# Three attention passes of one kernel: QKV signalled by halves, V rounded later, row-max work cut in half pieces with repeated products

## The reference, cut to what matters

```python
def fake_quant(x, bits=8):                      # per tensor
    qmax = 127.0
    scale = max(max(abs(x)) / qmax, 1e-8)
    return clip(round(x / scale), -128, 127) * scale

# quantised attention: B=8 batches, N=512 rows, 12 heads of 16
qkv  = fake_quant(x) @ fake_quant(w_qkv) + b_qkv
attn = fake_quant(softmax(fake_quant(q) @ fake_quant(k).T / 4))
out  = fake_quant(attn @ fake_quant(v)) @ fake_quant(w_proj) + b_proj
# routed stage, its attention: float32 throughout
q, k, v = layer_norm(x) @ qkv_w + qkv_b
x = x + softmax(q @ k.T / 4) @ v @ proj_w + proj_b
```

## Time and profile before

| | |
|---|---|
| median of 3 runs | 2557.32 us (2554.49 to 2562.55) |
| profiled execution | 2566.83 us |
| its span | 2564.8 us |
| PE busy | 1938.5 us, 76% |
| VectorE busy | 1504.3 us, 59% |
| ScalarE busy | 1058.4 us, 41% |
| GpSimd busy | 405.9 us, 16% |

### The profile page before, as it was taken

The page is one execution under the profiler, slowest core; times in us unless marked ns, Lnnn a source line. Parts: engine busy times, 40 slices in busy tenths (PEclk is TensorE's granted clock), DMA queues, the critical chain, the costliest instruction groups (busy, mean ns, idle before and its releaser), DMA issues. The chain is left out here.

```text
span 2564.8 us, 31153 instructions
## 1 busy us (share of the span) xinstructions
PE 1938.5 (76%) x9560; PEld 1006.8 (39%) x9560; DVE 1504.3 (59%) x2508; ACT 1058.4 (41%) x1847; POOL 405.9 (16%) x592
## 2 busy tenths in 40 slices
PE   5787888668785433777478865888899994899994
PEld 4555655444334110000111122333123332788883
DVE  6376389742104666999667773888968885111113
ACT  2002122132101356999678863222177761222221
POOL 5000000000111010111100003432003335122221
PEclk9899999766985665555589976777589996899997
DMA  3011100053991003333001004878767742565654
GB/s 79 18 31 37 48 23 25 2 223 125 410 411 42 0 0 124 119 119 119 28 16 36 25 1 68 131 96 107 93 75 96 99 59 77 178 212 194 212 195 183
DMA packets 147741, 265.16 MB, mean 103 GB/s; under 512 B 28618, under 2 KB 115883, under 8 KB 142636
## 3 DMA queue, kind: packets, MB, share of 16 engines
q1 hardware_dynamic: 135996, 242.54, 36.7%
q0 software_dynamic: 10480, 18.04, 2.1%
q10 hardware_dynamic: 1152, 3.15, 0.3%
HBM read 221.85 MB, written 57.71 MB: 109 GB/s over the span
## 5 line engine op out<-in xcount | busy, mean ns | idle before, releaser
L1654 PE MATMUL ps<-arena 128*128 x384 | 195.9, 615 | 121.7 <-DMA arena<-arena 62.2
L1688 ACT ACTIVATE ps<-ps,arena 128x512 f32<-128x512 f32 x384 | 256.6, 1451 | 7.7 <-POOL arena L1674 7.7
L2099 DVE TENSOR_REDUCE arena<-ps 128x1024 f32 x192 | 227.2, 1221 | 50.7 <-PE ps L2249 43.5
L1664 DVE TENSOR_REDUCE arena<-ps 128x1024 f32 x192 | 234.6, 1225 | 37.8 <-PE ps L1654 22.0
L1688 ACT ACTIVATION_READ_ACCUMULATOR ps<-ps,arena 128x1 f32 x384 | 239.7, 999 | 0.0
L2451 ACT ACTIVATE arena<-ps 128x1024 f32<-128x1024 f32 x192 | 185.2, 1021 | 95.8 <-PE ps L2333 94.6
L1838 ACT ACTIVATE arena<-ps 128x1024 f32<-128x1024 f32 x192 | 187.5, 1023 | 33.7 <-DVE arena L1860 29.4
L2781 DVE TENSOR_TENSOR arena<-ps,arena 128x384 f32<-128x384 f32 x39 | 21.7, 557 | 286.9 <-PE ps L2737 286.9
L2249 PE MATMUL ps<-arena 96*128 96x512 bf16 x384 | 159.6, 509 | 37.3 <-DVE arena L2099 24.6
L2761 ACT ACTIVATE arena<-ps,arena 128x256 f32<-128x256 f32 x234 | 89.5, 481 | 235.9 <-PE ps L2726 235.9
L528 PE MATMUL ps<-arena 96*128 96x456 f32 (+1 forms) x512 | 171.9, 486 | 8.7 <-DMA arena<-la_xt 5.1
(11 more groups left out here) (379 smaller groups left out, 3296.1 us busy)
## 6 DMA issues: line engine op xcount, KB each, us to landing
arena<-in_sm_w_dram SPq DMA_DIRECT2D x128, 576.0 KB
arena<-in_re_w_dram SPq DMA_DIRECT2D x39, 1252.0 KB, 6.0
arena<-ra_parts SPq DMA_DIRECT2D x192, 192.0 KB, 9.9
routed_in<-routed_in SPq DMA_DIRECT2D x8, 3332.0 KB, 13.8
ra_parts<-arena SPq DMA_DIRECT2D x48, 192.0 KB, 2.5
arena<-routed_in SPq DMA_DIRECT2D x39, 196.0 KB, 5.3
arena<-la_xt SPq DMA_DIRECT2D x16, 384.0 KB, 3.4
arena<-arena SPq DMA_DIRECT2D x64, 96.0 KB, 2.2
```

The costliest lines, as they stand in the source:

```text
L1654: ins = pe.matmul(ps[:, 2 * (n % 4) + t % 2, :], QM[j][:, h, t * P:(t + 1) * P], KI[:, b, h // HG, :], start=True, stop=True)
L1664: v.tensor_reduce(MXq[:, b, 2 * u:2 * u + 2, at_head(h)], ps[:, 2 * (n % 4):2 * (n % 4) + 2, :], AX.X, ALU.max).then_inc(s_lk, 1)
L1688: ins = act.activation(bank, bank, ACT.Exp, bias=nb[n % 4][:, t % 2:t % 2 + 1], scale=c_reg, accum_out=RS[:, b, t, at_head(h):at_head(h) + 1])
L2099: v.tensor_reduce(MX[:, bass.ds(b, 1), 2 * (n % 2):2 * (n % 2) + 2, n // 2].rearrange("p o t -> p (o t)"), ps[:, 2 * (n % 2):2 * (n % 2) + ...
```

## The change

Seven edits in the two stages.

1. *QKV.* The signal for q and k products counts two per batch, and PE's wait for free banks is per half. PE's order becomes q products, turn of b+1, k products, values, values. ScalarE scales the rows of b+2 between the copy of the turned rows and the store of k; two batches are scaled and rounded ahead of the loops. VectorE rounds b+2 after it has stored v.

```diff
-                qk.wait(act, b, 1)
+                qk.wait(act, b, k + 1)
...
             def batch(b, j, ahead):
-                if ahead:
-                    scale(b + 1)
                 store(b, 0)
                 if ahead:
                     turned(b + 1, 1 - j)
+                if ahead > 1:
+                    scale(b + 2)
                 store(b, 1)
...
-                ev.wait(pe, b, 0)
-                for s in range(2 * NG):
+                for k in range(2):
+                    ev.wait(pe, b, k - 1)
+                    for s in range(NG * k, NG * k + NG):
...
+                    ins.then_inc(qk.sem, 1)
+                    if ahead and k == 0:
+                        turn(b + 1)
                 values(b, j, 0)
-                if ahead:
-                    turn(b + 1)
                 values(b, j, 1)
```

```diff
+    tq, rq = Signal(nc, "qa_scaled", 3, 0), Signal(nc, "qa_rounded", 4, 1)
...
+                for n, (j, src, bias, k) in enumerate(((0, QF, magic, 0), (0, KF, magic_k, 1), (1, QF, magic, 0))):
+                    if n == 0:
+                        rq.wait(act, i, 0)
+                    elif n == 2:
+                        rq.wait(act, i, 1)
+                    act.activation(TM[n % 2], scaled(src, 2 * i + j), ACT.Identity, bias=bias,
+                                   scale=inv2[:, k:k + 1]).then_inc(tq.sem, 1)
...
+                v.tensor_scalar(TM[2], scaled(KF, 2 * i + 1), inv2[:, 1:2], magic_k, ALU.mult, ALU.add).then_inc(s_kt, 1)
```

```diff
+                Hb = m.H[:, b, :, :]
+                v.tensor_tensor(Hb, Hb, bp[:, None, :].to_broadcast([P, T, D]), ALU.add)
+            ex.wait(v, B - 1, N1)
+            l = Link(v, s_a)
+            l(v.tensor_reduce(pmax, RS, AX.XYZ, ALU.min))
+            v.reciprocal(pmax, pmax).then_inc(s_b, 1)
```

```diff
+    def shift_rows(eng, groups, done):
+        for q in groups:
+            for g in range(NG):
+                row, at = 32 * q + HD, 3 * (q * NG + g)
+                eng.dma_start(QI[row:row + 3, :, g, :], BT[at:at + 3, :, :]).then_inc(done, 16)
...
+            for b in range(2, B):
+                v.wait_ge(s_vt, b + 1)
+                round_v(v, b, TV[:, b, :].rearrange("p (h d) -> p h d", d=HD))
```

```diff
+            def pieces(b):
+                turns = [(turn, b + 1, c, half) for c in range(NC) for half in range(2)] if b + 1 < B else []
+                return [(product, b, s, half, c) for s in range(2 * NC) for half in range(2) for c in range(NC)] + \
+                    [(values, b, t) for t in range(2)] + turns + [(values, b, t) for t in range(2, T)]
+
+            def scores(b, j, n, again):
                 h = n // 2
                 mx.wait(pe, b, n - 1)
-                for t in (2 * (n % 2), 2 * (n % 2) + 1):
+                first = 2 * (n % 2)
+                for t in (first, first, first + 1) if again else (first, first + 1):
                     ins = pe.matmul(ps[:, t, :], ST_[j][0][0:KR, h, t * P:(t + 1) * P],
                                     ST_[j][1][0:KR, h, :], start=True, stop=True)
                 ins.then_inc(u1.sem, 1)
...
+                work = pieces(b + 2) if ahead else []
                 for n in range(NU):
-                    scores(b, b % 2, n)
-                    if ahead and 0 < n <= len(pieces):
-                        piece, *which = pieces[n - 1]
-                        piece(b + 2, *which)
+                    scores(b, b % 2, n, n < len(work) and work[n][0] is not values)
+                    if n < len(work):
+                        piece, *which = work[n]
+                        piece(*which)
...
+                act.activation(Vb[:, :, :, 1, :], m.one.to_broadcast([P, T * NH * HD]).rearrange(
+                    "p (t h d) -> p t h d", t=T, h=NH), ACT.Copy)
+                ins = act.activation(ST_[b % 2][1][KR:KR + 3, 3 * (b // 2):3 * (b // 2) + 3, :], m.one[KR:KR + 3].to_broadcast(
+                    [3, 3 * S]).rearrange("p (h s) -> p h s", h=3), ACT.Copy)
```

More of the change, by code:

```diff
@@ L1379, in _ @@
             pool.memset(WPf, 0.0).then_inc(s_z, 1)
+            pool.memset(magic_k, MAGIC)
+            pool.memset(above, MAGIC + 1.0)
             pool.memset(BQ, 0.0).then_inc(s_z, 1)
@@ L1496, in _ @@
             round_x(0)
-            with v.Fori(0, B - 1) as b:
+            round_x(1)
+            with v.Fori(0, B - 2) as b:
                 batch(b, True)
-            batch(B - 1, False)
+            for b in range(B - 2, B):
+                batch(b, False)
             v.wait_ge(s_lk, B)
@@ L1601, in _ @@
                 pool.memset(QM[j].rearrange("p h s -> p (h s)").bitcast(F32), 0.0).then_inc(s_qz, 1)
-        @block.sync
-        def _(sp):
-            sp.wait_ge(s_on, 1)
-            rq.wait(sp, B - 1, 3)
-            for j in range(HG):
-                rows = slice(32 * j + HD, 32 * j + HD + 3)
-                sp.dma_start(KI[rows].rearrange("p b g s -> p b (g s)"),
-                             ones[0:3, None, :].to_broadcast([3, B, NG * S])).then_inc(s_one, 16)
     RS, MXq = g3(P, [B, T, NH]), g3(P, [B, T, NH])
@@ L1617, in quantised_attention @@
     mark = g3.at
+    s_a, s_b, s_c, s_ln, s_bp, s_bt, s_bc, s_q = (sem(f"qa_shift_{n}") for n in (
+        "chain", "max", "max_of_all", "log", "parts", "turned", "copied", "rows"))
     nb = [g3(P, [2]) for _ in range(4)]
@@ L1697, in quantised_attention @@
     rows = lambda a: a.rearrange("p b t h -> p (b t) h")
-    s_a, s_b, s_c, s_ln, s_bp, s_bt, s_bc, s_q = (sem(f"qa_shift_{n}") for n in (
-        "chain", "max", "max_of_all", "log", "parts", "turned", "copied", "rows"))
+    s_q2 = nc.alloc_semaphore("qa_shift_rows_pool")
+    TV = QF.rearrange("p b g s -> p b (g s)")[:, :, 0:T * D]
     km = [sem(f"qa_k_spread{j}") for j in range(2)]
@@ L1741, in _ @@
                            ps[0:3 * NH, 2:4, :].bitcast(BF16), ACT.Copy).then_inc(s_bc, 1)
+            for b in range(2, B):
+                act.activation(TV[:, b, :], VF[:, b, :, :].rearrange("p t d -> p (t d)"), ACT.Identity, bias=magic,
+                               scale=inv2[:, 2:3]).then_inc(s_vt, 1)
         @block.tensor
@@ L2027, in _ @@
             v.wait_ge(s_w, 16 * (5 + HG))
-            v.memset(XT[DC:DC + 1, 0, :], 1.0)
+            for j in range(2):
+                v.memset(XT[j][DC:DC + 1, 0, :], 1.0)
         @block.scalar
@@ L2236, in values @@
                     rows = DC + 1 - c
-                    ins = pe.matmul(ps[:, 6 + t // 2, t % 2 * D:(t % 2 + 1) * D], XT[0:rows, c, t * P:(t + 1) * P],
-                                    W[0:rows, c, 2 * D:3 * D], start=(c == 0), stop=(c == NC - 1))
+                    ins = pe.matmul(ps[:, banks(b, 0) + t // 2, t % 2 * D:(t % 2 + 1) * D],
+                                    XT[b % 2][0:rows, c, t * P:(t + 1) * P], W[0:rows, c, 2 * D:3 * D],
+                                    start=(c == 0), stop=(c == NC - 1))
                 if t == T - 1:
                     ins.then_inc(qp.sem, 1)
-            pieces = [(turn, c) for c in range(NC)] + [(product, s, c) for s in range(2 * NC) for c in range(NC)] + \
-                [(values, t) for t in range(T)]
-            def scores(b, j, n):
+            def pieces(b):
[3 more added lines that the diff above has]
+            def scores(b, j, n, again):
                 h = n // 2
                 mx.wait(pe, b, n - 1)
-                for t in (2 * (n % 2), 2 * (n % 2) + 1):
+                first = 2 * (n % 2)
+                for t in (first, first, first + 1) if again else (first, first + 1):
                     ins = pe.matmul(ps[:, t, :], ST_[j][0][0:KR, h, t * P:(t + 1) * P],
@@ L2269, in batch @@
                             ins.then_inc(s_bt, 1)
+            for c in range(NC):
+                for half in range(2):
+                    turn(0, c, half)
             for b in range(2):
-                for piece, *which in pieces:
-                    piece(b, *which)
+                for piece, *which in pieces(b):
+                    piece(*which)
             for b in range(B):
```

176 lines of the change are left out of this document (90 added, 86 removed).

## The result

| | before | after |
|---|---|---|
| median of runs, us | 2559.94 (2554.49 to 2562.74, 4 runs) | 2474.34 (2473.01 to 2478.28, 4 runs) |
| span of the profiled execution, us | 2564.8 | 2473.2 |

The ratio is 0.9671, 95% interval 0.9655 to 0.9688: 3.3% faster. The forecast was 2487, range 2468 to 2516. The sum of -70 us was 15 too small; the median fell by 85.6 and the profiled span by 91.6 us.

A forecast was written before the change was run, and what follows sets the result against it. No engine was taken to bound the whole; stages were bound by chains or single engines. Terms -19 - 5.5 - 8 + 0.5 - 5 - 8 - 25.5 + 0.4 gave -70 us: 2487 as median, range 2468 to 2516.

The forecast's parts named there:

- QKV: QKV of the quantised attention: signalling products per half breaks the PE/ScalarE chain, leaving the longest engine; -19 us (-24 to -12).
- I take 7.6, at today's clock: QKV period per batch, down from 10.34 us: PE's 6.41 busy plus the gap between value products and hand-offs.
- What is late next is PE's own work: QKV after the change: PE itself, needing 7.6 us per batch with hand-offs, sets the period.
- Quantising and ones rows: Quantising loop's shorter chain, -5.5 us, and ones rows made by rounding bias, not issued by SP, -8: -13.5.
- Pass 1: Bias add moved here, eight VectorE adds of 0.96 us mostly absorbed by slack and ScalarE's queue: +0.5 (0 to +7.7).
- Shift block: Earlier GpSimd reconfiguring gains 1.3 us, twelve DMAs split over two queues, roundings of V added: -5 us (0 to -7).
- Projection: Projection loop loses the bias add and a short wait, period about 3.05 us: -8 us (-6 to -8.5).
- Routed pass: Routed row-max pass: halved pieces in all units, VectorE sets 28.8 us per batch; -25.5 us, memset +0.4.
- Rival 1: Clock stays at 1.2 GHz in the routed pass, so repeated products cost time: +47, 2604 us; chance 0.04.
- rival 2: Routed pass gains less: PE sets 1.30 us per unit, 32.4 per batch, -5 instead of -25.5: 2508 us; chance 0.15.
- rival 3: Small gains don't add up in QKV, shift block, bias add and quantising: 19 us less, 2506 us; chance 0.11.
- Rival 4: Memsets and moved waits give nothing, repeats cost a little: whole kernel within 0.3% of before; chance 0.02.

The follow-up runs named there:

- the third variant: Changed kernel without repeated score products in routed-pass batches 0 to 5, but with both score products repeated in batches 6 and 7: 2490.46 us, ratio 0.9705.

## Why the prediction was right, and where its sizes were off

**QKV (-19, measured -24.0).** The mechanism held: blocks of six products, ScalarE waiting 0.30 us for PE. The step "I take 7.6, at today's clock" was mis-sized. It let PE's 6.41 us set the period, and those were measured at 0.67. Once the chain was gone the clock was 1.00 in most of the stage, PE needs 4.08 there, and the period is 6.50; batches that ran partly at the lower level take up to 7.50, and only in those is the forecast's PE (busy 6.66) the longest engine. I had worked out VectorE's "6.6 to 7" and used it only as a bound. The variant with the short k maximum confirmed that VectorE is next, and ScalarE right behind it. "What is late next is PE's own work" was wrong for the batches at 1.00.

**Quantising and ones rows (-13.5, measured -14.8).** The pair's 6.91 us is the 6.9 of the chain. The ones rows gave 10.1 instead of 8: the four spreads take 3.12 us of issue, and with their landing and the block change 5.65 us in all, where I had left 7.6. The loop gave the other 4.7 instead of 5.5. The 5.5 was not the sum of its own terms, which is 4 x (8.92 - 6.9) - 3.5 = 4.6.

**Pass 1 (+0.5, measured +1.0).** With the add taken out again it is 0.6 to 1.4 shorter. ScalarE's records (line 1711) have a median of 1146 ns instead of the 1622 of the earlier trace rows, and 1622 again without the add, while the pace is the same. So the adds do shorten the work queued in them; that this pays for the delay, as forecast, is the reading that fits.

**Shift block (-5, measured -4.6).** Right in sum, wrong in both halves. The chain gained 2.8 us, not 1.3: I had put the block change and the table load behind GpSimd's reduction, but the other engines changed block while it still ran. After the copy I expected 7.8 us, set by the roundings, and it was 11.25: splitting the DMAs over two queues takes 4.8 us of issue away (9.74 to 4.94), but then the transfers are the bound. By its own terms the sum was 12.9 - 7.8 + 1.3 = 6.4; that 5 was put down, with 1.4 left unnamed, brought it near the 4.6, and that is luck. The rule of the Trainium skill, "SBUF — State Buffer" (SBUF: two separate sides), that was weighed against the change did not decide here. The Trainium skill, "GPSIMD Engine Reference" (section 2.1, Instruction dispatch), gives about 6 us for the first call of freshly loaded code; the 5.9 measured agree.

**Pass 2 (0, measured -1.8).** Its clock is 0.99 in place of the earlier trace rows's 0.97. The other traces with its new code have 220.9 to 223.3, so there is nothing to explain.

**Projection (-8, measured -8.1).** Period 3.09, forecast 3.05 to 3.1; confirmed by putting the add back (+7.7).

**Routed pass (-25.1 with the memset, measured -31.2).** VectorE sets the pace, as forecast, at 24 units of 1.13 to 1.14, not 1.15 (28.3 us per batch instead of 28.8, four batches: -2.0); batch 0 took 28.84 us, not 32, since the clock rose after two units and not five (-3.2); batch 5 has no norm of b+3 and took 27.20 (-1.6). Batch 0 was also added up wrongly: five units of 2.1, 19 of 1.15 and 1.24 are 33.6, not 32. These six fell from 201.5 to 169.3 us; the last two took 0.6 more, and 0.4 more lie ahead of the first reduction. What the prediction had wrong is the part of the repeated products: it gave them a share in holding the clock, and without them the time is the same. What holds it is the spread of the pieces, which the prediction had only as a shorter unit.

**The rivals.** Rival 1 is refuted by 1.00 in the middle batches, rival 2 by 28.3 us per batch (it had 32.4; its -5 for the pass is -3 to -4 by its own terms, which changes nothing), rival 3 by the sum of the small gains: QKV, quantising, pass 1, shift block and projection together are -50.5 against its forecast of -26. Rival 4 does not come into it.

**The sum.** -70 forecast, -85.6 in the medians. Two terms were too small: QKV by 5, priced at the lower clock, and the routed pass by 6, from the sizes above. Another 6 us of the profiled difference can't be told from scatter. The other terms were each within 1.3 us, in the shift block by errors that cancel.

## What to carry to other kernels

When a chain is broken, price the next bound with each engine's work at both clock levels: a PE block measured in a stalled stage is dearer than it will be. When PE feeds a reader at a fixed pace, cut its side work so that every unit carries an equal piece; padding it with repeated products brought nothing here and, in units without pieces, cost 13 us. Sharing small copies over two queues saves issue time only until the transfers themselves end last, as they did here at 11.25 us after the copy. And where a stage scatters by 3.7 us between executions of the same code, a gain of 3 us in it must be read batch by batch.

## What the runs showed of the hardware that was not expected

- Nearly full PE work doesn't bring the higher level by itself: 0.50 with PE busy 36.82 of 39.00 us of score products, 1.00 with PE busy 24.51 of 28.30 us when each unit holds a piece of the float32 QKV work between its score products, and 0.76 with the same work bunched in half of the units. In the third variant it was 0.50 for 31 us of unbroken work and then 0.99.
- In this kernel other engines pass the end of a block while GpSimd is still reconfiguring for a reduction over partitions: ScalarE's table load began at 1217.08 us, the reduction at 1220.10.
- Twelve copies of three partitions each kept a mean share of 0.20 of 16 DMA engines; with half of the bytes and rows the median time to landing of GpSimd's six fell from 5.0 to 2.0 us, more than in proportion.
- VectorE's roundings of 128x768 took 0.62 to 0.64 us while GpSimd issued DMAs and 0.54 to 0.55 afterwards; the DMAs were not slowed.
